# Linear attention with routed experts on one NeuronCore: a new hand-written statement order for three engines' loops and tails, with two semaphore waits added

## The reference

```python
    x = x + _L1_attn_ref(_layernorm(x, axis=-1), ...)   # x: 8 batches, 256 tokens, 256 wide
    x = x + _L1_ffn_ref(_layernorm(x, axis=-1), ...)
...
    q = short_conv(hidden_states @ Wq, conv_wq)   # 4 taps, then silu; k and v alike; 6 heads, 32 keys, 64 values
    beta = jax.nn.sigmoid(hidden_states @ Wb)
    g = -jnp.exp(A_log) * jax.nn.softplus(hidden_states @ Wa + dt_bias)
    # for each token: S = S * exp(g); delta = (v - k S) * beta; S = S + k delta; o = q S
    o = o * jax.lax.rsqrt(jnp.mean(o * o, -1, keepdims=True) + EPS) * norm_weight
    o = o * jax.nn.silu(gate)
    return o.reshape(b, t, VALUE_DIM) @ Wo
```

## Time and profile before

| | us |
|---|---|
| median of 3 runs | 1187.88 (1187.67 to 1191.72) |
| the profiled execution, whole | 1189.71 |
| its span on the engines | 1188.0 |
| PE busy in the span | 1117.4 (94%) |
| DVE busy | 836.5 (70%) |
| ACT busy | 638.3 (54%) |
| mean granted TensorE clock, share of full speed | 0.935 |

### The profile page before, as it was taken

How to read it: one execution, slowest core, us unless ns; L and a number is a source line. 1 busy time by engine, 2 the same in 40 slices (tenths; PEclk the granted TensorE clock), 3 DMA queues, 4 the chain that set the end, 5 groups by cost and what they waited for, 6 DMA issues and landing times. The chain is left out here.

```text
span 1188.0 us, 26425 instructions
## 1 busy us (share of the span) xinstructions
PE 1117.4 (94%) x9990; PEld 960.0 (81%) x9990; DVE 836.5 (70%) x2423; ACT 638.3 (54%) x1615; POOL 213.2 (18%) x246
## 2 busy tenths in 40 slices
PE   6999999999999998999999999759799999899898
PEld 4898899889989997888888888647587777677687
DVE  5777467647855775868676766799877887797353
ACT  5644444444444443554433344457867787777462
POOL 0422222222213222430000000121102211220010
PEclk9999999999999998999999999968877887897699
DMA  9200000000000002001000000100000001000323
GB/s 309 85 2 2 1 1 1 1 1 1 1 1 1 1 1 80 19 1 29 1 1 1 1 1 1 59 30 32 25 10 33 31 2 33 33 1 3 100 67 103
DMA packets 26702, 32.91 MB, mean 28 GB/s; under 512 B 4960, under 2 KB 21968, under 8 KB 26576
## 3 DMA queue, kind: packets, MB, share of 16 engines
q1 hardware_dynamic: 26576, 31.22, 8.4%
HBM read 29.04 MB, written 2.17 MB: 26 GB/s over the span
## 5 line engine op out<-in xcount | busy, mean ns | idle before, releaser
L333 DVE TENSOR_TENSOR a_ps<-a_ps,causal 128x256 f32<-128x256 f32 x128 | 54.7, 427 | 92.6 <-PE a_ps L642 92.6
L1547 PE MATMUL b_ps<-ln_high,b_high 128*128 128x512 f32 x256 | 102.0, 398 | 1.1 <-ACT gate_up_raw L1462 1.1
L692 PE MATMUL a_ps<-a_wo_high,a_oT 128*128 128x256 f32 x512 | 101.3, 282 | 0.1
L1547 PE MATMUL b_ps<-ln_low,b_high 128*128 128x512 f32 x256 | 101.2, 395 | 0.0
L1547 PE MATMUL b_ps<-ln_high,b_low 128*128 128x512 f32 x256 | 100.7, 393 | 0.0
L316 POOL TENSOR_TENSOR a_probs<-a_probs,a_inv 128x256 f32<-128x256 f32 x64 | 40.1, 627 | 330.6 <-DVE a_inv L353 330.6
L1581 PE MATMUL b_ps<-b_wd_high,b_mid 128*128 128x256 f32 x512 | 97.9, 286 | 0.0
L494 ACT ACTIVATE a_probs<-a_ps,a_negmax 128x128 f32<-128x128 f32 x128 | 47.0, 367 | 89.4 <-DVE a_negmax L339 76.6
L508 ACT CAST a_oT<-a_ps 128x512 fp32r<-128x512 f32 x64 | 37.5, 587 | 107.0 <-PE a_ps L670 107.0
L1462 ACT ACTIVATE gate_up_raw<-b_ps 128x512 f32<-128x512 f32 x64 | 37.5, 598 | 94.9 <-PE b_ps L1547 94.8
L1347 DVE TENSOR_TENSOR gate_up_raw<-gate_up_raw,b_ps 128x512 f32<-128x512 f32 x64 | 42.9, 685 | 61.8 <-ACT gate_up_raw L1462 32.0
(11 more groups left out here) (435 smaller groups left out, 3064.9 us busy)
## 6 DMA issues: line engine op xcount, KB each, us to landing
gate_up_raw<-a_scratch SPq DMA_DIRECT2D x8, 768.0 KB, 3.7
gate_up_raw<-in_D_main SPq DMA_DIRECT2D x8, 304.5 KB
x<-in_hidden SPq DMA_DIRECT2D x4, 512.0 KB, 11.1
a_raw<-in_A_q SPq DMA_DIRECT2D x4, 512.0 KB, 8.8
gate_up_raw<-in_A_o SPq DMA_DIRECT2D x1, 2048.0 KB
gate_up_raw<-in_B_g SPq DMA_DIRECT2D x1, 2048.0 KB, 12.1
gate_up_raw<-in_B_u SPq DMA_DIRECT2D x1, 2048.0 KB, 9.5
out<-x SPq DMA_DIRECT2D x8, 256.0 KB, 2.7
```

What stands on the lines that cost most here:

```text
L333: nc.vector.tensor_tensor(diagonals, diagonals, r.causal[:].rearrange("p (o k) -> p o k", o=1).to_broadcast([P, 2, P]), ALU.add).then_inc( ...
L692: mm = nc.tensor.matmul(ps[:, out_bank(job), 0:HID], opart, wpart, start=(k == 0 and j == 0), stop=(k == QUARTER - 1 and j == len(passes) ...
L1547: mm = nc.tensor.matmul(ps[:, bank, :], wpart, xpart, start=(j == 0), stop=(j == len(passes) - 1))
```

## The change

All statements of the three loops and tails stay; they stand in another order, and the tails too. PE gets two waits. `gates` of batch 0 waits for the copies of an earlier transpose out of the bank that it shares. `job` 4 now stands ahead of `solve`, and its bank is also that of `corner`, so it waits until ACT has copied that out. The diff, of the tables only a line or two:

```diff
@@ vector loop
+                    last(m, statistics, 0)
+                    run(m, products, 2)
+                    run(c, convolve, 2, 3)
+                    last(m, newton, 0)
...
-                    last(m, statistics, 0)
-                    run(m, products, 2)
-                    run(m, products, 3)
-                    last(d, pairs.add, dve, 0)
...
@@ scalar loop
+                    run(c + 1, scan_starts, 2, DH)
                     run(s, save_output, 0)
-                    run(m, copy_low, 2)
                     run(s, squares, 1)
-                    run(c + 1, scan_starts, 0, 2)
+                    run(c, silu, 3)
+                    run(c, silu, 4)
...
                 def gates(m, k):
                     if m == 0:
                         pe.wait_ge(late_loaded, 16 * LATE_LOADS)
+                        if GATE_BANKS[k] in TURNED_BANKS:
+                            pe.wait_ge(n3.copied, DC * (GROUPS - n3.start // GROUP_TILES))
...
                 def job(c, j):
                     if j == 0:
                         pe.wait_ge(S["conv_step"], at("conv_step", c - 1, (TAPS - 1) * 4))
+                    if j == 4 and c >= 2:
+                        pe.wait_ge(S["inverse_done"], at("inverse_done", c - 2, 2))
```

More of the change, by code:

```diff
@@ L2467, in _ @@
                     c, m, s, d = t + 1, t, t - 1, t - 2
+                    run(m, products, 0)
+                    run(m, products, 1)
+                    if t == 1:
+                        late.logarithms(dve)
+                    run(c, convolve, 0, 1)
+                    run(c, convolve, 1, 2)
+                    last(m, statistics, 0)
+                    run(m, products, 2)
+                    run(c, convolve, 2, 3)
+                    last(m, newton, 0)
+                    run(c, convolve, 3, 4)
+                    last(s, statistics, 1)
+                    run(m, products, 3)
+                    run(s, join_pairs)
                     if t == 0:
@@ L2482, in _ @@
+                    run(m, products, 5)
                     run(c, convolve, 4, 5)
[L2483 removed]
                     run(m, keys_by_token)
[L2485 removed]
                     run(c, convolve, 5, 6)
                     run(c, scan, 0)
[L2488 to L2490 removed]
                     run(c, scan, 1)
[L2492 to L2493 removed]
@@ L2810, in _ @@
                     run(s, copy_part16)
-                    last(s, rt.exponential, act, 0)
-                    run(m, second_keys)
+                    if t == 1:
+                        late.exponential(act)
+                    run(m, values_by_token, 0)
+                    run(c, silu, 0)
                     last(m, norm_root, 0)
                     run(s, place_second)
+                    run(m, second_keys)
+                    run(m, fold_even)
+                    last(s, norm_root, 1)
@@ L2825, in _ @@
                     run(c, tap, 3)
                     run(d, copy_oT, 0)
+                    run(d, copy_oT, 1)
                     run(s, place_corner)
-                    last(s, norm_root, 1)
-                    run(d, copy_oT, 1)
-                    if t == 1:
-                        late.exponentials(act)
-                    run(c, square_of, 0)
+                    run(m, copy_low, 0)
+                    run(c, square_of, 1)
+                    run(c + 1, scan_starts, 0, 2)
                     run(m, copy_low, 1)
-                    run(c, silu, 1)
@@ L2847, in _ @@
+                    last(m, norm_copy, 0, 0)
+                    run(c, silu, 2)
+                    run(c, tap, 4)
+                    run(s, copy_wkT)
+                    run(c, square_of, 2)
                     run(c, tap, 5)
-                    run(c, square_of, 2)
-                    run(s, copy_wkT)
-                    if t == 1:
-                        late.exponential(act)
                     run(s, squares, 0)
```

207 lines of the change are left out of this document (99 added, 108 removed).

## The result

The changed kernel takes 1202.4 us (median of 4 runs, 1199.1 to 1205.1) against 1188.9 for the kernel before on the same chip: ratio 1.011, 95% interval 1.008 to 1.014. It is slower by 1.1%, and 29 us above the forecast of 1173. The profiled execution took 1203.0 us with a span of 1201.3, where before it was 1188.0, 13.3 less.

What follows compares the result with a forecast made beforehand. A middle iteration was bound by the larger of DVE's 36.4 us and PE's 34.5 to 39.3 plus 0.8, depending on PE's clock. Gains 13.5 + 1 + 0 + 3 - 1 = 16.5 off 1189.7 gave 1173 us, range 1157 to 1190.

Steps and rivals of the forecast that it cites:

- the term of 13.5 us: Iterations 2 to 6: half of PE's half-clock stretch goes, period 38.2 us, gain 2.7 each, 13.5 for five.
- two of three pauses go: PE around `pair_inverses`, iterations 2 to 6: dense work between small matmuls removes two pauses before the clock's fall.
- iteration 1: `logarithms` moves behind `products` 1: one PE stall of 3.75 us goes, one of 3 comes; gain 1, between -3 and 4.
- iteration 7: Waits of 2.84 us at `products` 4 and 1.71 ahead of `logits` 0 go, `newton` costs 0.7; gain 3, bounds 0 and 5.
- rival 1: Clock stays up in the middle iterations, by fewer pauses and dense work between: 26 us off, 1162 us; chance 0.2.
- PE's need: PE's busy time in a middle iteration: 34.5 us at full clock, 39.3 with the slow stretch as it is.
- DVE's leg: DVE's bound on a middle iteration: 33.1 us busy plus 3.3 of remaining waits, 36.4 us.
- The fourth table load: ACT, ahead of `silu` 0 and `place_second`: 1.28 us per iteration, covered by 3.45 us of idle time.
- rival 4: Slower: the fourth table load and `fold_even` ahead of `copy_part32` land on the ring of waits; 1199 us, chance 0.1.
- The slow stretch's price: PE's 13.3 us at half clock in iteration 3 valued at 4.8 us, from the work lying in it.
- Iteration 8 and tail: `norm_root` and lost cover for `solve` cost time, earlier weight transfers may help; 1 us lost, between loss 3 and gain 2.
- Iteration 0: DVE puts `products` ahead of the layer norm's `newton`, total unchanged; gain 0, within 1 us either way.

Runs made afterwards that it cites:

- g1: Changed kernel with SP's 768 KB transfer split from `spread` and issued early, once the batch before's scans are done: ratio 0.9893 to the kernel before, 1177.4 us.
- e3: Changed kernel with the 768 KB transfer (`spread`) of iterations 2 to 6 issued only when `pair_inverses` is done: ratio 0.9935 to the kernel before, 1181.1 us.
- e4: Changed kernel with ACT's tap 3 put ahead of `copy_part64`: ratio 1.0088 to the kernel before.
- n2: Changed kernel with the 768 KB transfer issued early and ACT's tap 3 ahead of `copy_part64`: ratio 0.9928 to the kernel before.
- n3: Changed kernel with the 768 KB transfer issued early and PE's `scores` 4 back behind `quarter_part`: ratio 1.0133 to the kernel before.
- f4: Changed kernel with iteration 1's `logarithms`, `exponentials` and `exponential` at their old places and `late.turn` behind `outputs` 1: ratio 1.0096 to the kernel before.
- n4: Changed kernel with the 768 KB transfer issued early, iteration 1's three late statements and `late.turn` back at their old places: ratio 0.9880, 1175.4 us.
- e2: Changed kernel with DVE's `keys` put back ahead of `column_product` 15: ratio 1.0037 to the kernel before, 1194.0 us.
- g2: Kernel before with the 768 KB transfer split from `spread` and issued once the batch before's scans are done: ratio 0.9989 to the unmodified kernel before.

## Why the prediction was wrong

**The step that failed** is the term of 13.5 us, "I take half of the slow stretch away", from what PE did before the fall: two of three pauses go. They went, and a pause without a releaser of 1.3 to 2.5 us, for which the sum has no term, came into `pair_inverses` in their place. In place of 13.5 gained, iterations 2 to 6 lost 7.0; with iteration 1 (5.6 worse than its term) and iteration 7 (4.7 worse) that is the distance to the forecast within 1 us. The prediction says nothing of `keys`, though POOL's `decayed_keys` and SP's 768 KB hang on it. With that transfer out of the way (g1 and e3) the ratio is 0.989 and 0.9935: rival 1's mechanism, for part of the iterations, and the forecast's sign.

**What the trace of before already showed.** Pauses of this kind stood within its bursts in iterations 5 and 6: 0.90, 0.95, 0.69 and 0.98 us, each 2.2 to 2.4 us behind the start of a packet. The prediction took iteration 1 as a sign that `pair_inverses` without a pause keeps the clock; that reading is wrong, since the same iteration has one inside it, kernel before:

```profile
820.16 0.67 PE L2994 MATMUL c_ps<-cb_inv,cb_part 32*32 32x32 f32 x45 [0.68 <-issue]
```

**The legs were right at full clock.** PE's need: 34.5 forecast, 34.46 busy in g1. DVE: 36.4 forecast (33.1 busy and 3.3 of waits), 36.13 and 36.24 in g1 with 32.7 busy. DVE's leg, the longer of the two, is the period when the clock stays up. Its sum is in part luck: the largest wait in g1's iteration 4, 1.32 us ahead of `products` 0 for `scores` 0, is not among the pieces that the prediction names. In the changed kernel PE has no pause ahead of `quarter_inverses` or `job` 4 in iterations 2 to 6, and `known` waits for nothing; at full clock (g1) there are 0.30 ahead of `quarter_inverses`, within the forecast's 0.5. The fourth table load is covered in iterations 3 to 6, where ACT still waits 1.06 to 2.24 us for DVE ahead of `place_second`. So rival 4 had the right side with a mechanism that did not happen. The load took 1.28 us, as the row has it.

**The slow stretch's price.** I valued it by what it cost where it stood. It can move: at about the same length in all (64.6 and 67.2 us in iterations 2 to 6) PE was busy nearly 6 us longer with the same work, as it came over the dense part. Where the stretch stood before, the price was right: 4.8 forecast, and 39.2 busy before against 34.46 in g1.

**The DVE leg** missed the wait for tap 3, 3.3 us, where 3 to 3.5 were left for everything. e4 and n2 show no gain from taking it away. That `scores` 4 must not stand behind `quarter_part` was right: in n3 its return cost 2.4%, more than any other move that was tried alone.

**Iteration 1.** Forecast a gain of 1, between -3 and 4; lost 4.6. The pause of 3 near `join_pairs` came, 4.02 us; the step that is missing is the move of `late.turn` ahead of `outputs` 1, 3.78 us. f4's trace, at 43.9 us, says that both together are the loss; n4's, with the same statements back at 47.4, does not bear it out, so the split stays open.

**Iteration 7.** Forecast a gain of 3, lost 1.7. The waits of the earlier trace rows did go: `products` 4 waits 1.31 in place of 2.84, and none stands ahead of `logits` 0. But the clock fell behind a pause of 1.65 without a releaser and was at half for 20 us in one piece; before, it was at half for 17 and 3 us. In n4, where it was at half for 7 us only, this order takes 36.3 us, 3.7 less than before, so the term is right at that clock. What made the slow stretch shorter there is not shown: n4's pause is longer, 2.06. **Iteration 8 and tail**: 1 lost forecast, 0.8 measured; the pieces of that term were not tested one by one. **Iteration 0**: forecast 0, won 0.9.

**Open.** That the late transfer lengthens the pause is shown; what brings the clock down is not, beyond that it kept up in most of the new order's iterations without the pause (4 and 5 of g1, 2 to 5 of e3 and n4). It fell in iteration 3 of g1 without one, and in iteration 2 of g1 with 0.84, where iterations 2 and 4 of e2 kept it with 0.87 and 0.85. What makes the clock fall in the old order even with the transfer away (g2) was not parted from the density of its work. Why f4's shorter iteration 1 does not show in its runs, and does not come back in n4, is open as well.

## What to carry to other kernels

When a statement moves, follow what waits for it through every engine to the DMA queues, and look where the transfer then lands: a burst of 168 tiny matmuls had to wait here for its own instructions, which came through the same DMA engines. A pause that the profile gives to "issue" in the middle of such a burst is a first suspect, and holding the transfer back took one wait (e3). Before valuing a reordering at the clock seen in one trace, ask which work the slow stretch will lie over once the order has changed.

## What the runs showed of the hardware

- Packets of 16 KB on an instruction queue go with PE's pauses; PE went on 2.4 us after the packet began in the changed kernel (991.68 to 994.05) and in g1 (982.35 to 984.74). With 768 KB ahead of it, the packet came 2.1 us later against the burst.
- A pause lies at a fixed place of the stream, 16 matmuls further in each iteration, and it can reach 1.32 to 2.06 us with hardly any DMA traffic (iterations 6 and 7 of g1 and n4).
- Not every pause given to "issue" is one of these: the 1.71 ahead of `logits` 0 in the kernel before came 7.9 us behind the last packet of q8.
- PE's clock stayed at 2.4 GHz through iterations with pauses of 0.87 and 0.85 us in the burst (e2). In iterations 2 to 6 of the changed kernel it fell during each pause of 1.3 to 2.5 us or within 3 us of its end; but it fell also where there was none (iteration 3 of g1).
- A middle iteration of the new order took 36.13 and 36.24 us at full clock (iterations 4 and 5 of g1), 40.8 to 43.9 in the changed kernel.
